# Two experts per token: dense expert stage against token lists scattered through DRAM

## What is computed

```python
scores = jnp.einsum('btd,de->bte', x, router_w)
probs = jax.nn.softmax(scores, axis=-1)
routing_weights, routing_idx = jax.lax.top_k(probs, 2)
routing_weights = routing_weights / jnp.sum(routing_weights, axis=-1, keepdims=True)
one_hot = jax.nn.one_hot(routing_idx, 8)
expert_w = jnp.einsum('btke,btk->bte', one_hot, routing_weights)
dispatched = jnp.einsum('btd,btke->bted', x, one_hot)
gate = jnp.einsum('bted,edf->btef', dispatched, gate_proj)   # d = 128, f = 352
up = jnp.einsum('bted,edf->btef', dispatched, up_proj)
expert_out = jnp.einsum('btef,efd->bted', jax.nn.silu(gate) * up, down_proj)
return jnp.einsum('bted,bte->btd', expert_out, expert_w)
```

## Time and profile before

| | us |
|---|---|
| median of 3 runs | 2134.11 (2132.44 to 2137.86) |
| the profiled execution's own time | 2140.14 |
| its span, first to last instruction | 2138.3 |
| PE busy | 2001.0 (94%) |
| mean granted TensorE clock | 0.964 of full speed |

### The profile page before, as it was taken

One profiled execution on the slowest core, in us unless ns is written; L12 is line 12 of the kernel. 1 busy time (PEld: TensorE's weight loads), 2 busy tenths in 40 slices (PEclk: granted clock), 3 DMA queues, 4 the chain that ended last, 5 costly groups with the idle time before them and its releaser, 6 DMA issues. The chain is left out here.

```text
span 2138.3 us, 31115 instructions
## 1 busy us (share of the span) xinstructions
PE 2001.0 (94%) x11744; PEld 886.3 (41%) x11744; DVE 1462.6 (68%) x2435; ACT 1184.2 (55%) x2372; POOL 142.2 (7%) x216
## 2 busy tenths in 40 slices
PE   4599999999999999999998799999999999999876
PEld 2244444444436666666665212222222222222355
DVE  5577777777724554545555978888888888886276
ACT  2246666666662222322232337777777777777776
POOL 3100000000000000000000100000000000000165
PEclk9689999999999999999999769999999999999998
DMA  7633423433000000000000411001111110100000
GB/s 206 135 38 42 51 36 43 49 37 45 2 2 1 1 1 1 1 1 1 1 1 6 112 15 16 16 16 17 21 24 17 16 16 16 16 2 1 1 16 25
DMA packets 75268, 56.70 MB, mean 27 GB/s; under 512 B 43120, under 2 KB 57328, under 8 KB 75120
## 3 DMA queue, kind: packets, MB, share of 16 engines
q1 hardware_dynamic: 64416, 38.62, 12.9%
q0 software_dynamic: 3072, 10.23, 1.4%
q10 hardware_dynamic: 7632, 5.88, 1.0%
HBM read 38.65 MB, written 12.32 MB: 24 GB/s over the span
## 5 line engine op out<-in xcount | busy, mean ns | idle before, releaser
L1140 DVE TENSOR_REDUCE rowmax<-ps 128x1 f32<-128x1024 f32 (+7 forms) x1024 | 970.2, 987 | 245.3 <-PE ps L559 125.1
L909 ACT ACTIVATE probs<-ps 128x512 f32<-128x512 f32 (+3 forms) x1792 | 857.5, 557 | 338.6 <-PE ps L592 215.1
L559 PE MATMUL ps<-K,Q 72*128 72x512 bf16 (+3 forms) x1792 | 539.3, 376 | 27.8 <-DVE rowmax L1140 24.1
L592 PE MATMUL ps<-Q,K 75*128 75x512 bf16 (+3 forms) x1792 | 535.8, 361 | 12.9 <-ACT probs L909 8.7
L608 PE MATMUL ps<-probs,V 128*9 128x512 f32 (+3 forms) x3584 | 443.7, 552 | 0.0
L592 PEld LDWEIGHTS ps<-Q,K 75*128 75x128 bf16 x1792 | 165.3, 98 | 365.5 <-ACT probs L909 268.1
L945 ACT ACTIVATE Q<-ps 128x512 f32<-128x512 f32 (+1 forms) x192 | 114.4, 596 | 323.7 <-PE ps L718 312.1
L559 PEld LDWEIGHTS ps<-K,Q 72*128 72x128 bf16 x1792 | 152.4, 99 | 315.4 <-DVE rowmax L1140 166.4
L1251 DVE TENSOR_TENSOR Q<-ps,Q 128x512 f32<-128x512 f32 (+1 forms) x192 | 130.5, 687 | 141.5 <-PE ps L721 140.8
L721 PE MATMUL ps<-Q,wu 128*128 128x512 f32 (+1 forms) x384 | 196.7, 594 | 1.6 <-DVE Q L1251 1.6
L718 PE MATMUL ps<-Q,wg 128*128 128x512 f32 (+1 forms) x384 | 196.9, 594 | 0.7 <-DVE attn L1165 0.7
(11 more groups left out here) (157 smaller groups left out, 1122.6 us busy)
## 6 DMA issues: line engine op xcount, KB each, us to landing
Q<-q_parts SPq DMA_DIRECT2D x288, 64.0 KB
K<-k_parts SPq DMA_DIRECT2D x144, 64.0 KB
q_parts<-Q POOLq DMA_DIRECT2D x16, 384.0 KB, 3.4
k_parts<-Q POOLq DMA_DIRECT2D x8, 384.0 KB, 7.3
V<-v SPq DMA_DIRECT2D x16, 144.0 KB
K<-k_parts SPq DMA_DIRECT2D x144, 16.0 KB
x<-in_L_attn_h_dram SPq DMA_DIRECT2D x4, 512.0 KB, 10.1
out_dram<-y SPq DMA_DIRECT2D x8, 256.0 KB, 2.3
```

What stands on the lines that cost most here:

```text
L559: last = pe.matmul(buf[:, c:e], Q[0:CROSS, slot, j, i * P:(i + 1) * P], K[0:CROSS, slot, kj, c:e], start=True, stop=not diag)
L592: last = pe.matmul(ps[:, bank, c:HALF], K[0:KROWS, q, kj, t * P:(t + 1) * P], Q[0:KROWS, q, j, h * HALF + c:(h + 1) * HALF], start=True, s ...
L909: act.activation(probs[:, (4 * m + j) % PR, c:HALF], ps[:, B_BANKS[(4 * m + j) % 3], c:HALF], ACT.Exp, scale=SCALE).then_inc(sl["exp_done" ...
L1140: dve.tensor_reduce(rowmax[:, par, 8 * j + i:8 * j + i + 1], score_a(i % 2)[:, 0:hd.keys(i)], AX, ALU.max).then_inc(sl["max_done"], 1)
```

## The change

The experts see only the tokens that picked them. The tokens are worked in two groups `g` of four blocks (`NGRP`, `GU`).

- Routing (`route`) is a table of steps per engine. For group 0 steps 0 to 11 stand at the 12 probability-times-V events of the last attention quad, the rest behind it; for group 1 they stand in the tiles of group 0, three tiles apart. `rank_experts` also counts; a product with a triangular matrix of ones (`PF`) gives each token its place in each expert's list, `place_rows` the row numbers, `tile_table` the expert and first row of each tile.
- `scatter_rows(u)` on POOL writes each token's normed row, with 8 pairs of (target, weight) behind it (ROW = 144 floats), twice into `dispatch[g]` in DRAM: 8 indirect transfers of 128 rows for each block.
- `experts` runs 39 tiles of 128 rows for each group, 78 in all, whatever the lists hold. SP reads first row and expert of a tile into registers and issues two loads (rows, and target with weight). PE turns the tile, multiplies it with the expert's gate and up weights (352 columns each), turns the product in three pieces and multiplies down. ACT scales by the weight, POOL scatters the rows to `returned` in DRAM. There are TS = 4 buffers for loaded and for finished tiles.
- `load_back(u)` and `combine(u)` add both results of each token to x; for group 0 within the tiles of group 1, for blocks 4 to 7 at the end.
- During attention(0), POOL fills the lists (18 transfers of 16 x 128 rows), so that rows that no token wrote are numbers.

```diff
-    "tensor": [{1: (0, 0), 3: (0, 1), 6: (0, 2), 8: (0, 3)}, ...
+ROUTE = {
+    "tensor": [steps([("T2", 5), ("WO", 2), ("T1", 0), ("LG", 6), ("PF", 9)], 1, 0, ("TOT", 13)),
...
+    "gpsimd": [steps([("RS", 2), ("SC", 10)], 1, 0, None), steps([("RS", 2), ("SC", 10)], 3, 1, None)],
...
+            def load_tile(g, t):
...
+                if n >= TS:
+                    sp.wait_ge(ex["turned"], n - TS + 1)
+                    sp.wait_ge(ex["y_ready"], n - TS + 1)
+                    sp.wait_ge(ex["target"], n - TS + 1)
+                row = sp.value_load(row_of[0:1, g, t:t + 1], min_val=0, max_val=(E + 1) * CAP - P)
+                expert = sp.value_load(expert_of[0:1, g, t:t + 1], min_val=0, max_val=E - 1)
+                sp.dma_start(x_tile[:, k, :], dispatch[g][bass.ds(row, P), 0:D]).then_inc(tile_in[k], 16)
+                sp.dma_start(meta[:, k, :], dispatch[g][bass.ds(row, P), bass.ds(expert * 2 + D, 2)])\
+                    .then_inc(tile_in[k], 16)
...
+            def scatter_rows(u):
...
+                for choice in range(2):
+                    for k in range(GT):
+                        at = bass.IndirectOffsetOnAxis(ap=index[:, v, choice, k:k + 1], axis=0)
+                        pool.indirect_dma_start(dispatch[u // GU][:, :], at, rows[:, v, k, :], None)\
+                            .then_inc(scattered[v], 16)
...
+            def scatter_tile(n):
...
+                pool.indirect_dma_start(returned[:, :], at, y_tile[:, k, :], None,
+                                        bounds_check=2 * B * S - 1, oob_is_err=False).then_inc(tile_out[k], 16)
...
-            def gate_up(u, e):
...
-            def down(u, e):
...
+            def turn_tile(n):
+
+                k = n % TS
+                pe.wait_ge(tile_in[k], 32 * (n // TS + 1))
+                if n >= 1:
+                    pe.wait_ge(ex["h_ready"], n)
+                if n >= 4:
+                    pe.wait_ge(ex["y_ready"], n - 3)
...
+            def down_tile(n):
...
+                pe.wait_ge(ex["act_ready"], n + 1)
+                pe.wait_ge(ex["h_ready"], min(n + 4, NGRP * TILES))
...
+                for n in range(NGRP * TILES):
+                    expert = gate_tile(n)
+                    if n + 1 < NGRP * TILES:
+                        turn_tile(n + 1)
+                    up_tile(n, expert)
+                    if n >= 1:
+                        turn_acts(n - 1)
+                    if n >= 2:
+                        down_tile(n - 2)
+                    if n < TILES:
+                        route(1, n)
...
+                for n in range(NGRP * TILES):
+                    if n >= 3:
+                        weigh_tile(n - 3)
+                    gate_tile(n)
+                    if n + 1 < NGRP * TILES:
+                        take_tile(n + 1)
...
+            def combine(u):
...
+                own.done(dve.tensor_tensor(xs, xs, y_in[:, par, :, 0, :], ALU.add))
+                tell(dve.tensor_tensor(xs, xs, y_in[:, par, :, 1, :], ALU.add), y_taken, u + 1)
+                statistics_rms(u)
```

More of the change, by code:

```diff
@@ new lines, with numbers @@
+LAST = 24
+SINES = 24
+BACK, TAKE = (5, 8, 11, 14), (8, 11, 14, 17)
+def numbers(engine, kinds):
+    tables, n = [], 0
+    for g in range(NGRP):
+        table = {}
+        for step in sorted(ROUTE[engine][g]):
+            for ev in ROUTE[engine][g][step]:
+                if ev[0] in kinds:
+                    table[ev], n = n, n + 1
+        tables.append(table)
+    return tables
+TURNS = numbers("tensor", ("T1", "T2"))
+SMALL = numbers("tensor", ("WO", "LG", "PF", "TOT"))
+READS = numbers("vector", ("ADD", "SH", "IDX", "TAB"))
@@ L685, in attention @@
                 pe.wait_ge(sl["attn_done"], 2 * NQ + AT_ONE)
[L687 to L710, removed]
@@ L808, in _ @@
             attention(0)
-            for u in range(NG - 1):
-                experts(u, True)
-            experts(NG - 1, False)
+            for step in range(LAYERS[0].G, LAST):
+                route(0, step)
+            experts()
             project(1)
@@ L938, in experts, with route @@
-            def experts(u, more):
-                for e in range(E):
-                    for c, (f, w) in enumerate(FCH):
-                        n = 3 * (E * u + e) + c
-                        par = (3 * e + c) % 2
-                        act.wait_ge(moe["gate"], n + 1)
-                        act.wait_ge(moe["mul"], n + 1)
-                        act.activation(gated[0:w, par, :], ps[0:w, par, :], ACT.Silu).then_inc(moe["silu"], 1)
-                    if more and e in (1, 5, 7):
-                        prepare(u + 1, e // 2)
-                    if not more and e == 4:
+            def route(g, step):
+                first = (1, 6)[g]
+                for kind, u in ROUTE["scalar"][g].get(step, ()):
+                    if kind == "EX":
+                        act.wait_ge(pre["small_read"], READS[g]["SH", u] + 1)
+                        if u >= 2:
+                            act.wait_ge(pre["picked"], u - 1)
+                        act.activation(exped[:, u % 2, :, :], shifted[:, u % 2, :, :], ACT.Exp).then_inc(pre["exped"], 1)
+                        continue
+                    act.wait_ge(pre["turned"], COPIES[g][kind, u] + 1)
+                    if u >= 1:
+                        before = {"CP1": "WO", "CP2": "LG"}[kind], u - 1
+                        act.wait_ge(pre["small"], SMALL[(u - 1) // GU][before] + 1)
+                    act.activation((aT if kind == "CP1" else hT)[:, :], ps[:, first, :], ACT.Copy)\
+                        .then_inc(pre["copied"], 1)
```

581 lines of the change are left out of this document (439 added, 142 removed).

## The result

The changed kernel takes 2290.68 us (median, 2289.01 to 2297.84) beside 2135.99 us of the kernel before on the same chip: ratio 1.0733, 95% interval 1.0704 to 1.0761. It is 7% slower, although PE does less work. The forecast was 2307 us.

A forecast was written before the change was run, and what follows sets the result against it. PE's arithmetic was taken to bound the expert stage before the change. Start 45 + 78 tiles x 8.0 + end 31 = 700 us in place of 527.5 gave a 2310.8 us span, less 4.2: 2307 us, range 2070 to 2430.

The forecast's parts named there:

- PE is spared 321 us: Expert stage: PE's products fall from 500 us to 179 us for 78 tiles; PE alone would gain 320 us.
- The ring: Each tile: a whole load lies between one down product and the next turning, 4.6 us (3.2 to 6.3) outside PE.
- The register reads: SP's two reads before each tile's load, in series: 0.7 us each, 1.4 together (0 to 1.7).
- Half clock: PE in the tiles: load waits keep its clock at half, 3.4 us of work instead of 1.7; chance 0.48.
- T: Time per tile in the expert stage: 4.6 + 3.4 = 8.0 us (6.6 to 9.7).
- The start: Before the first tile turns: POOL's 32 indirect transfers at 1.1 us, then landing and loads; 45 us (35 to 60).
- The end: After the last tile: scatter, load, then blocks waiting in turn for POOL's inverse roots, 6.0 us each; 31 us.
- At nothing: Costs taken as hidden: group 1's routing, POOL's scatters, group 0's combine, and the fills (up to 10 us if delaying row maxima).
- Full clock: Rival for the tiles: PE keeps full clock, 6.3 us a tile, 2174 us; chance 0.29.
- Short load: Rival for the tile loads: cheap reads, quick landing, PE keeps its clock; 4.9 us a tile, 2065 us; chance 0.12.
- Dear scatters: Rival for POOL's indirect transfers: 3 us each, start grows by 61 us, about 2370 us; chance 0.11 (or worse).
- Work not cut: Rival for the experts: work not cut as said; held excluded by the order's fixed 78 tiles, no chance given.

The follow-up runs named there:

- Eight buffers: The changed kernel with eight instead of four buffers for loaded and finished tiles: 1951.5 us, ratio 0.9138 to the kernel before.
- the run with dead work: The changed kernel with six unread float32 products per tile between gate product and next turning, keeping PE busy: 2194.7 us, ratio 1.0295.
- the half: The changed kernel with row scatters for each token's first expert only, 16 transfers instead of 32 before the first tile: 2254.5 us, ratio 1.0550.
- `meta` alone: The changed kernel with eight buffers for meta (target and weight) only, row buffers staying four: 1967.1 us, ratio 0.9207.
- The run with T = 5.93: The changed kernel with SP's two register reads moved ahead of its wait for the weighing: 2159.2 us, ratio 1.0104.

## Why the prediction held, point by point

- **PE is spared 321 us.** Eight buffers show less: PE's own tile is 2.88 us, not 2.3, which leaves 275. The sum left out 0.1 each in gate and down, 0.17 of draining behind down, and 0.23 of issue ahead of each gate, where PE fetches its own expert number. This was hidden in a ring of 7.5 us. In a kernel with enough buffers it would have been 45 us of error.
- **The ring.** Right, and the main step. Handover and weighing 0.42 (0.5 said), two reads 1.2 (1.4), row issue with what stands around it 0.5 (0.4), second transfer 1.64 to 1.84 with its own issue 0.2 ahead (2.3). In sum 4.0 to 4.2 in the tiles shown and 4.3 on the average (4.6). The term most off is the landing: the row of 2.3 was a transfer of 256 KB written out, and the small load lands about 0.5 us sooner (1.8 by the issues' median). The prediction named a landing "well under 2 us" as a sign of being wrong; it came half true and cost the forecast little.
- **The register reads.** The reads took 0.6 us each. The Trainium skill ("DMA: Bandwidth & Descriptors", Latency and other measured facts) has this floor. The trace comes near it for a whole read, not for the load instruction alone: 0.26 of load, 0.16 of register work and the gaps make 0.57, and two reads more cost 1.06 us a tile. Taking its figure would have given 2291 instead of 2307; that this is the measured time to the microsecond is luck, since larger differences in other terms cancel.
- **Half clock.** PE's part of a tile is 3.45 us on the average, the 3.4 forecast. The clock was not near 0.5 throughout, as the prediction had it: the windows show 0.68 on average, because it is often up while PE waits. (PE was busy 59% of the stage, as the prediction's signs had it.) It was 0.50 from 902 to 911 us, 1.00 from 912 to 914, with PE idle, and 0.50 again at 915. The rule of the Trainium skill ("TensorE: Matmul & The Clock Gate", Loop structure matters more than you think) decided rightly between the rivals, and the run with dead work shows its price here: 96 us. 133 were said, by 1.7 us a tile; measured were 1.40 in group 1 (at full clock PE's part takes 2.05 us where 1.7 was said) and 1.24 over both groups.
- **T.** 7.6 us, 8.0 said: the tiles took 32 us less in all. Only half of that is the size of the ring (7.76 us a tile from the fourth on). The sum multiplied by 78, but the first four tiles find empty buffers: their loads do run ahead, and the first three steps took 2.5 us each, 16 us less than three rings. The start took back 6, the later stages 3 (in the first 20 us of the next projection the granted clock is 0.68, before it was 0.84), and the median stands 3.5 us above the profiled span where 4.2 below it was taken, which is 8: together the 16 us between 2307 and 2291. That the forecast was only 0.7% off is in part luck: the errors of single terms went both ways.
- **The start.** 51 us, 45 said. POOL's transfers are 0.96 and a gap of 0.30, 1.27 in all where 1.1 was taken: 32 x 0.17 = 5 us. That they and not DVE bind is shown by the half. POOL's first transfer stands at 640.3, as forecast, but by luck: this execution was some 4 us ahead, so the routing of the three more blocks took that much longer than said.
- **The end.** 30.7, 31 said; its pace of 6.0 us a block was 6.43. Right as a chain through POOL.
- **At nothing.** Group 1's routing: T is 7.65 in the later tiles of group 0 and rises to 8 and 9 in single tiles of the routing, balanced by others of 6; from the fourth tile to the twentieth it costs about 5 us in all. At full speed it would not be free: eight buffers give T 3.22 on average where a bare tile is 2.88. The POOL scatters fit at T 7.5, and don't at 2.9 (`meta` alone). The fills cost nothing that shows: from PE's first product of P times V to the one shown at 569.80 us are 452.0 us, and 452.5 in the kernel before.
- **Break-even.** It was put at T = 5.8. The run with T = 5.93 was 1.0% slower, which agrees to 12 us.
- **The rivals.** Full clock: no; made by force it gives 2195 (2174 said). Short load: the trace has 4.3 us outside PE, just above its limit of 4.1, and PE does not keep the full clock that it supposed. Dear scatters: 1.27 us, no. Work not cut: PE's busy time fell by 158 us.

## What to carry to other kernels

Follow each buffer from its load to its last reader, the smallest too, and count how many steps of the loop lie between: if the next load into it waits for a step that itself waits for the item just loaded, the whole latency stands in every round, and here 4 KB more for the smallest buffer were worth more (324 us) than the arithmetic that the change removed from PE (275). Work out the round both ways (latencies in series over buffers, and the busy time of every engine), and take the greater; an edit that costs latency in one costs only occupancy in the other (81 against 31 us here). Engine work that can be done ahead of a wait, such as reading addresses into registers, belongs ahead of it.

## What the runs showed of the hardware

- **Clock and short waits.** With PE waiting 3.2 us in a round of 7.6 the mean granted clock of the stage was 0.66 to 0.70; with 2.0 in 6.0 (reads before the wait) 0.76; with 0.6 in 6.3 (PE kept busy) 1.00. In the first two it goes between its levels of 1.2 and 2.4 GHz inside a tile, and the mean says little of the work: at 0.68 PE's part of a tile took 3.45 us, where a tile at 0.50 throughout took 3.57 and one at 1.00 2.05.
- **Small loads landed in 1.8 us** in this stage (median of 78 each), 128 pieces of 512 B as well as 128 pieces of 8 B. At the changed kernel's start, where 202 GB/s moved, single loads of 0.5 to 4 KB took 2.9 to 5.5 us.
- **SP's work for one tile** (two reads, two transfers with computed addresses) is 2.3 us where nothing holds it (the first tiles with eight buffers), of which only 0.7 are the transfers' issue in the trace.
- **Indirect transfers** of 128 rows cost POOL 0.96 us and a gap of 0.30, and land after 2.3 to 2.5 us; a plain issue of the kernel before was 0.77.
